# A feed-forward over a tree of 255 nodes: one merged table for the low levels, tiles in pairs, overflow groups of 128 rows

## The reference

```python
for _ in range(DEPTH + 1):                    # 8 levels, nodes 0 to 254
    score = einsum('td,td->t', flat_x, w1s[current]) + b1s[current]
    current = current * 2 + choice + 1        # choice: score > 0
path_weights = gelu(abs(logits))              # one weight per row and level
for i in range(DEPTH + 1):
    t_i = einsum('td,tdo->to', flat_x, w2s[nodes_i]) + b2s[nodes_i]
    out = out + t_i * path_weights[:, i][:, None]
```

## Time and profile before

| | |
|---|---|
| median of 3 runs | 547.82 us (547.79 to 549.1) |
| profiled execution | 548.32 us, its span 546.5 us |
| busy: PE, DVE, ACT, POOL | 378, 366, 300, 277 us |
| attention's last scores | near 338 us |
| first static product, first row-out | 412.6, 418.3 us |
| last row-out issued, end of span | 537.7, 546.5 us |

### The profile page before, as it was taken

How to read it: one execution, slowest core, us unless ns; L and a number is a source line. 1 busy time by engine, 2 the same in 40 slices (tenths; PEclk the granted TensorE clock), 3 DMA queues, 4 the chain that set the end, 5 groups by cost and what they waited for, 6 DMA issues and landing times.

```text
span 546.5 us, 8746 instructions
## 1 busy us (share of the span) xinstructions
PE 378.2 (69%) x3014; PEld 251.9 (46%) x3014; DVE 366.0 (67%) x594; ACT 299.8 (55%) x655; POOL 277.4 (51%) x315
## 2 busy tenths in 40 slices
PE   1333859888898988988588993556109996587780
PEld 1222525444465645655355651554007774354450
DVE  0644495878867789687888788625956999443341
ACT  2463767999888998889588694002001110254440
POOL 1456594322236287362677506838375777741211
PEclk9999996999999999999799996655558999599996
DMA  5202497397330333302331300750014110200000
GB/s 130 65 1 54 114 229 150 86 196 131 86 86 14 73 86 86 86 22 65 85 85 34 86 1 4 129 84 4 16 35 109 40 43 22 73 9 5 7 5 7
DMA packets 52029, 36.03 MB, mean 66 GB/s; under 512 B 25122, under 2 KB 50687, under 8 KB 51980
## 3 DMA queue, kind: packets, MB, share of 16 engines
q1 hardware_dynamic: 48238, 32.47, 27.4%
q0 software_dynamic: 2944, 2.45, 1.7%
q10 hardware_dynamic: 800, 0.49, 0.4%
HBM read 10.57 MB, written 8.79 MB: 35 GB/s over the span
## 4 chain that ended last, share of the span: by engine, by line
ACT 29%; PE 26%; DVE 25%; issue 8%; POOL 6%; DMA 3%; ACTq 0%; SPq 0%; POOLq 0%; DVEq 0%
ACT S L943 15%; PE S L735 5%; DVE nm L1097 5%; PE U L674 5%; DVE lm L1268 4%; DVE vT L1261 3%; ACT q L930 3%; ACT vT L930 3%; PE S L838 3%; ACT k L930 3%; DMA par<-in_L_tok_moving_var 2%; PE U L838 2%; POOL pool_a L459 2%; PE S L840 1%; POOL w L452 1%
## 5 line engine op out<-in xcount | busy, mean ns | idle before, releaser
L1097 DVE TENSOR_REDUCE nm<-S 128x1 f32<-128x748 f32 x192 | 171.9, 932 | 44.7 <-PE S L735 41.9
L943 ACT ACTIVATE S<-S,nm 128x748 f32<-128x748 f32 x192 | 167.1, 885 | 42.6 <-DVE nm L1097 41.4
L735 PE MATMUL S<-pool_a 128*128 128x512 f16 (+1 forms) x768 | 151.6, 332 | 29.6 <-ACT S L943 27.1
L735 PEld LDWEIGHTS S<-pool_a 128*128 128x128 f16 x768 | 68.9, 105 | 91.7 <-ACT S L943 56.2
L550 POOL DMA_INDIRECT out<-lm,vT x44 | 43.4, 985 | 58.1 <-DVE lm L1274 51.1
L459 POOL TENSOR_TENSOR pool_a<-q,pool_a 128x750 f16<-128x750 f32 x16 | 25.8, 1613 | 72.3 <-DVE pool_a L1064 72.1
L635 PE MATMUL U<-xhT,wq 128*128 128x250 f16 x288 | 42.9, 289 | 17.7 <-ACT q L930 8.2
L1268 DVE TENSOR_REDUCE lm<-vT 128x64 f32<-128x512 f32 x44 | 45.1, 1026 | 1.6 <-DVE vT L1261 0.5
L943 ACT ACTIVATION_READ_ACCUMULATOR S<-S,nm 128x1 f32 x192 | 44.0, 229 | 0.0
L635 PEld LDWEIGHTS U<-xhT,wq 128*128 128x128 f16 x288 | 27.1, 104 | 35.5 <-ACT q L930 13.7
L491 POOL DMA_INDIRECT sorted_rows<-xrow,slot x24 | 26.9, 1119 | 18.4 <-DVE slot L1183 10.3
(11 more groups left out here) (214 smaller groups left out, 681.6 us busy)
## 6 DMA issues: line engine op xcount, KB each, us to landing
pool_a<-pool_a SPq DMA_DIRECT2D x64, 187.5 KB, 3.0
pool_a<-pool_a SPq DMA_DIRECT2D x64, 93.8 KB, 2.8
sorted_rows<-zrow SPq DMA_DIRECT2D x1, 3864.0 KB, 22.3
vT<-sorted_rows SPq DMA_DIRECT2D x11, 276.0 KB, 3.7
w<-in_L_ffn_w2s SPq DMA_DIRECT2D x1, 2048.0 KB
lm<-in_x SPq DMA_DIRECT2D x4, 375.0 KB
pool_a<-in_L_ffn_w2s SPq DMA_DIRECT2D x1, 1024.0 KB
out<-lm,vT POOLq DMA_INDIRECT x44, 2.1
```

The source lines that it names most:

```text
L735: last = mm(S[n % 3][:, c0:c1], kst[:, u % 3, a, hd, START[t]:START[t] + P], qst[:, u % 3, hd, c0:c1], start=(a == 0), stop=(a == 1))
L943: sc_.activation(S[n % 3][:, 0:N], S[n % 3][:, 0:N], ACT.Exp, bias=nm[:, b % 2, j, i:i + 1], accum_out=sm[:, b % 2, j, i:i + 1]).then_inc( ...
L1097: v.tensor_reduce(nm[:, b % 2, j, i:i + 1], S[n % 3][:, 0:N], X, ALU.max, negate=True).then_inc(s_max, 1)
```

## The change

Rows, order of the sort and results stay. What differs:

- Overflow groups have 128 rows (`P`) instead of 32, so a group is a tile with one leaf. 96 groups stay provided for: 96 tiles, `SLOTS` from 7168 to 16384.
- Static and overflow tiles go in pairs: one load, one transpose step, one PSUM tensor of 1024 columns and one VectorE step for two tiles. Overflow blocks under an `If` are one pair: 48 of them.
- Levels 0 to 5 lie in one table `wlow` of 32 x 6 entries, level 6 in `w6` behind it (256 entries instead of 160, 15 transfers instead of 19, twice). A static tile has seven products (384, 2 x 64, 4 x 64 columns), an overflow tile three of full height (384, 64, 64). ACT's copies to `yv` are gone.
- The reduction over levels becomes three additions (4+4, 2+2, 1+1 levels).
- The fill goes in four pieces, behind the stacks of units 1 to 4; `w7` behind those of unit 5. `q32`, `k32`, `xhT` and `wq` move into `pool_a`; the low tables also wait for the last q-k product.
- POOL issues the writes of batch 2 ahead of the wait for the last scores and of the clearing, which covers 16,384 elements instead of 10,368.
- Transposes of a pair are issued one pair ahead, the first overflow pair's before the last static pair's products; PE's wait for the group numbers comes at the third pair.

```diff
-SLOTS = STAT + OVG * G
-ST_TILES, OV_TILES = STAT // P, OVG * G // P
+SLOTS = STAT + OVG * P
+ST_TILES, OV_TILES = STAT // P, OVG
+FILLS = 4
+ST_PAIRS, F_PAIRS = ST_TILES // 2, F_TILES // 2
+NODES5 = 2 ** 5
+LOWN = 6 * NODES5
...
-                if w == 1:
+                if 1 <= w <= FILLS:
                     sp.wait_ge(s_id, 2)
-                    sp.dma_start(rows.rearrange("(t p) c -> p t c", p=P),
-                                 zrow[:].unsqueeze(1).to_broadcast([P, F_TILES, RW])).then_inc(s_fill, 16)
-                if w == 4:
+                    fl = slice((w - 1) * F_TILES // FILLS, w * F_TILES // FILLS)
+                    sp.dma_start(rows.rearrange("(t p) c -> p t c", p=P)[:, fl, :],
+                                 zrow[:].unsqueeze(1).to_broadcast([P, F_TILES // FILLS, RW])).then_inc(s_fill, 16)
+                if w == FILLS + 1:
...
             sp.wait_ge(s_score, 2 * NT * NU)
+            sp.wait_ge(s_prod, NU)
...
+                for lv in range(6):
+                    n = 2 ** lv
+                    r = NODES5 // n
+                    m = D if src is wv else 1
+                    if n <= r:
+                        for i in range(n):
+                            sp.dma_start(tv[rows_, i * r:(i + 1) * r, lv, :],
+                                         src[:, n - 1 + i:n + i, :].to_broadcast([m, r, D])).then_inc(s_low, 16)
+                    else:
+                        for q in range(r):
+                            sp.dma_start(tv[rows_, q::r, lv, :], src[:, n - 1:2 * n - 1, :]).then_inc(s_low, 16)
...
+            load_rows(ST_PAIRS)
             groups = sp.value_load(nact[0:1, 0:1], min_val=0, max_val=OVG)
-            for k in range(ST_TILES // 4, F_TILES // 4):
-                with sp.If(groups > 4 * (4 * k - ST_TILES)):
-                    load_rows(k)
+            for m in range(ST_PAIRS, F_PAIRS - 1):
+                with sp.If(groups > 2 * (m - ST_PAIRS)):
+                    load_rows(m + 1)
...
+            own_slots(B - 2)
             pool.wait_ge(s_score, 2 * NT * NU)
-            link(gp.memset(wlow[D:P, :], 0.0))
+            link(gp.memset(pool_a[D:P, 0:n_low + 2 * NODES5 * D], 0.0))
             pool.sem_inc(s_zl, 1)
             pool.wait_ge(s_uf, unit_no[("o", B - 1, 1)] + 1)
             link(gp.memset(xsT[D:P], 0.0))
             pool.sem_inc(s_zl, 1)
-            own_slots(B - 2)
             own_slots(B - 1)
...
+            def overflow_pair(m):
+                leaves = [nc.tensor.value_load(lami[0:1, 2 * (m - ST_PAIRS) + t:2 * (m - ST_PAIRS) + t + 1],
+                                               min_val=0, max_val=LEAVES - 1) for t in range(2)]
+                pair_ready(m)
+                for t in range(2):
+                    y = y_banks(m)[:, 512 * t:512 * (t + 1)]
+                    xk = xsT[:, m % 3, t * P:(t + 1) * P]
+                    mm(y[:, 0:6 * D], xk, wlow[:, bass.ds((leaves[t] >> 2) * (6 * D), 6 * D)], start=True, stop=True)
+                    mm(y[:, 6 * D:7 * D], xk, w6[:, bass.ds((leaves[t] >> 1) * D, D)], start=True, stop=True)
+                    last = mm(y[:, 7 * D:8 * D], xk, w7[:, bass.ds(leaves[t] * D, D)], start=True, stop=True)
+                last.then_inc(s_y, 1)
...
             xs_T(0)
+            for m in range(ST_PAIRS):
+                if m == 2:
+                    pe.wait_ge(s_goff, 1)
+                xs_T(m + 1)
+                static_pair(m)
             groups = pe.value_load(nact[0:1, 0:1], min_val=0, max_val=OVG)
+            for m in range(ST_PAIRS, F_PAIRS):
+                with pe.If(groups > 2 * (m - ST_PAIRS)):
+                    if m + 1 < F_PAIRS:
+                        xs_T(m + 1)
+                    overflow_pair(m)
...
+            def weigh(m):
+                dve.wait_ge(s_gelu, m + 1)
+                dve.wait_ge(s_y, m + 1)
+                wk = xs[:, m % NX, :, C_W:C_H]
+                v.tensor_tensor(wy[:, m % 2], y_banks(m)[:].rearrange("p (t l o) -> p t l o", t=2, l=DEPTH),
+                                wk.unsqueeze(3).to_broadcast([P, 2, DEPTH, D]), ALU.mult).then_inc(s_wy, 1)
...
+            for m in range(ST_PAIRS):
+                weigh(m)
+                if m >= 1:
+                    levels_1(m - 1)
+                levels_4(m)
+                if m >= 1:
+                    add_residual(m - 1)
+                levels_2(m)
...
+            for m in range(ST_PAIRS, F_PAIRS):
+                with dve.If(groups > 2 * (m - ST_PAIRS)):
+                    weigh(m)
+                    levels_4(m)
+                    levels_2(m)
+                    levels_1(m)
+                    add_residual(m)
```

More of the change, by code:

```diff
@@ L358, in _ @@
             for k in range(ST_TILES - NO, ST_TILES):
                 sp.wait_ge(s_outr[k % NO], 16 * (k // NO + 1))
-            for m in range(ST_TILES // 4, F_TILES // 4):
-                with sp.If(groups > 4 * (4 * m - ST_TILES)):
-                    for k in range(4 * m, 4 * m + 4):
+            for m in range(ST_PAIRS, F_PAIRS):
+                with sp.If(groups > 2 * (m - ST_PAIRS)):
+                    for k in range(2 * m, 2 * m + 2):
                         sp.wait_ge(s_outr[k % NO], 16 * (k // NO + 1))
@@ L497, in own_slots @@
                 if b == 0:
-                    pool.wait_ge(s_fill, 16)
+                    pool.wait_ge(s_fill, 16 * FILLS)
                 pool.wait_ge(s_slot, b + 1)
@@ L556, in _ @@
                     scatter(FIRST + k, oslot, s_sego)
-            for m in range(ST_TILES // 4, F_TILES // 4):
-                with pool.If(groups > 4 * (4 * m - ST_TILES)):
-                    for k in range(4 * m, 4 * m + 4):
+            for m in range(ST_PAIRS, F_PAIRS):
+                with pool.If(groups > 2 * (m - ST_PAIRS)):
+                    for k in range(2 * m, 2 * m + 2):
                         rows_out(k)
@@ L848, in _, with pair_ready @@
-            pe.wait_ge(s_goff, 1)
-            xs_T(0)
-            for k in range(ST_TILES):
-                if k % 4 == 0 and k + 4 < ST_TILES:
-                    xs_T(k // 4 + 1)
-                tile_products(k)
-            groups = pe.value_load(nact[0:1, 0:1], min_val=0, max_val=OVG)
-            for m in range(ST_TILES // 4, F_TILES // 4):
-                with pe.If(groups > 4 * (4 * m - ST_TILES)):
-                    xs_T(m)
-                    pairs = load_leaves(4 * m)
-                    for k in range(4 * m, 4 * m + 4):
-                        pairs = overflow_products(k, pairs)
+            def pair_ready(m):
+                pe.wait_ge(s_xc, m + 1)
+                if m >= NY:
+                    pe.wait_ge(s_wy, m - NY + 1)
@@ new lines, in levels_1, with add_residual @@
+            def levels_1(m):
+                for k in range(2 * m, 2 * m + 2):
+                    if k >= NO:
+                        dve.wait_ge(s_outr[k % NO], 16 * (k // NO))
+                dve.wait_ge(s_s2, m + 1)
+                w = wy[:, m % 2]
+                v.tensor_tensor(yo_pair(m), w[:, :, 0, :], w[:, :, 1, :], ALU.add).then_inc(s_sl, 1)
+            def add_residual(m):
+                dve.wait_ge(s_sl, m + 1)
+                o = yo_pair(m)
+                v.tensor_tensor(o, o, xs[:, m % NX, :, C_H:C_ID], ALU.add).then_inc(s_yo, 1)
```

240 lines of the change are left out of this document (84 added, 156 removed).

## The result

The changed kernel takes **554.66 us** (median, 553.51 to 555.58) against 547.81 us for the kernel before in the same comparison: ratio 1.0117, 95% interval 1.0096 to 1.0138, so slower by about 1.2%. The prediction was 556.0. The profiled execution took 553.51 us around a span of 551.8, the one before 548.32 around 546.5, so in the traces there are 5.3 us to place.

The account below looks back on a forecast made before the run. Waits, not busy engines, bound it: GpSimd's queue, then TensorE's walk. First row-out +8.8, last overflow write +10.8, last row-out -0.7, end +8.2: span 554.7, plus 1.8 less 0.5 gives 556.0 us; range 542 to 571.

Parts of the forecast that it names:

- Slots of batch 3: Start of the stage: a VectorE operation stands still beside GpSimd's longer clearing, so the slots come 5.4 us later.
- The end of 12.4 us: Upper bound of the slots' delay, if VectorE's two-input operations also stood still beside the clearing: 12.4 us.
- First row-out at 427.1: GpSimd's first row-out, behind slots, loads, first tiles and VectorE's steps: 427.1 instead of 418.27, +8.8 us.
- The GpSimd loop: Alternating row-outs and overflow writes: same 36 instructions, 45.0 us, plus 2 (0 to 5) beside VectorE's sums; last overflow write 474.1.
- Step of 3.1 in the overflow pairs: Overflow stage: 14 steps between pairs at 3.1 us each (ends 2.8 and 3.9), together 43.4 us.
- The walk: End of kernel: TensorE steps over 33 unused blocks, fetching code, in 22 us, ending at 554.2; bounds 5 and 134 us.
- the span ends with that: Kernel before: TensorE's steps over three unused blocks, 3.4 to 5.0 us each until 546.0, set the end of the span.
- The +8.2 of the end: End of the span: TensorE's walk ends at 554.2 and the span at 554.7, +8.2 us on the kernel before.
- Rival 1: TensorE's queue: sequencing costs nothing, step 2.8 us, last row-out 532.8, total time 544.1 us, faster by 0.7%; chance 20%.
- Rival 2: Cheap walk at the end but step 3.1: last row-out 537.0, SyncE 547.0, total time 548.3 us, no change; chance 12%.
- Rival 3: Score units: the fills delay the stacks of units 4 to 6, +7 us on the forecast, 563; chance 12%.
- Rival 4: Walk at the end: every step over a block costs a fetch, 134 us instead of 22, total 668 us; chance 6%.

Follow-up runs that it names:

- experiment 2: Changed kernel with the clearing of pool partitions 64 to 127 moved from GpSimd to ScalarE: 549.46 us, 1.0015 to the kernel before.
- experiment 3: Changed kernel with batch 2's row writes put back behind GpSimd's clearings, the clearing keeping its new size: 551.70 us, 1.0055 to the kernel before.
- Experiment 7: Changed kernel with the three additions put back to one reduction in the 16 static pairs only: 550.22 us, 1.0037 to the kernel before.
- experiment 6: Kernel before with room for 48 overflow groups instead of 96, so no block is stepped over: 548.03 us, 0.9997 to the kernel before.
- experiment 4: Changed kernel with all 24 overflow writes of GpSimd issued before its first row-out: 543.35 us, 0.9905 to the kernel before.
- Experiment 5: Kernel before with all 24 overflow writes of GpSimd issued before its first row-out: 545.87 us, 0.9958 to the kernel before.
- experiment 9: Kernel before with room for 48 groups and all overflow writes first: 570.68 us, 0.9889 to a kernel before at 577.0 in that session.
- experiment 10: Changed kernel with six more indirect GpSimd writes into a table nobody reads: 591.19 us, 1.0250 to the kernel before in that session.
- experiment 1: Changed kernel with conditional code for 16 overflow blocks beyond the static pair instead of 47: 552.75 us, 1.0081 to the kernel before.
- experiment 8: Changed kernel with the clearing on ScalarE and overflow writes first: 537.52 us, 0.9799; with static-pair reduction too: 563.62 us (0.9777), repeated 535.85 us (0.9775).

## Why the prediction was right or wrong

- **Slots of batch 3, +5.4.** Right in place, cause and size: 5.5 us, and experiments 2 and 3 show the cause. The end of 12.4 us is out: two-input operations and a reduction ran beside the clearing as always. The rule of the Trainium skill (SBUF — State Buffer, § SBUF: two separate sides) by which the delay was 5.4 agrees with this trace, where L271 with its two SBUF inputs took 0.95 us beside the clearing.
- **First row-out at 427.1.** It came at 426.89, and 1.5 us later where TensorE's clock rose later.
- **The GpSimd loop, +2 for the additions.** The term was mis-sized: the loop took 49.3 us instead of 45.0, +4.2, inside the bounds of 0 to 5 and near their upper end. Experiment 7 gives the 4.4 back.
- **Step of 3.1 in the overflow pairs.** 3.07 measured, but the reason was half right. I had three bounds at 2.8 to 3.0, on VectorE, on TensorE's sequencer and in its array, and counted the stage on TensorE; VectorE's own chain (2.92 us busy, the rest between dependent sums) sets it, and GpSimd is stretched to the same 3.07. TensorE's last product ends at 527.5, 4.7 us before the predicted 532.2, since three pairs of PSUM banks let it run ahead of VectorE, which I forgot. First products 12 us after the last overflow write instead of 14.7 made up for part of the longer loop. Last row-out 538.50 for 537.0.
- **The walk.** For TensorE I had 22 us, and it took 15.6: four steps of 1.6 to 2.1 us where I had six or seven of about 3, the others 0.20 to 0.35, most 0.21. The instruction queue brought five packets of 16 KB in that time (525 to 542), which fits fetches. What failed is the step "the span ends with that". It was wrong for the kernel before (experiment 6), so also for the changed one: GpSimd's drain, which I put at 550.6, ended at 551.5, TensorE's walk at 541.5 instead of 554.2. The two lay 0.3 us apart in the trace of before, and I took TensorE's, the earlier one, for the cause. The +8.2 of the end should have been built from GpSimd: its 33 steps behind VectorE's last sum, or the end of its last row-out if that is later, and then its drain.
- **Rivals.** Rivals 1 and 2 let the walk of TensorE be cheap or hidden; for the span it was hidden. Rival 2 had the last row-out at 537.0 (538.5) and SyncE through at 547.0 (546.2), and still gave 548.3, since I let it end with SyncE and left out the drain that I had put at 550.6 a paragraph earlier; with it, it would have been the better forecast of the mechanism. Rival 1's step of 2.8 us did not occur. **Rival 3** (fills) falls: the fills take 15.2 us each beside the stacks, and the first scores of each unit come between 0.2 us earlier and 0.6 us later than before. **Rival 4** falls with 29 of 33 steps at 0.20 to 0.35 us, most at 0.21; the Trainium skill (Advanced Engine Details and Errata, § Control Flow Timing) gives about 108 ns for a compare-and-branch, half of the 208 measured.

So the sum of 556.0 came near 554.66 partly by luck. From the last row-out to the end I had 17.7 us (537.0 to 554.7) where the trace has 13.3 (538.50 to 551.8), and those 17.7 were built on the wrong queue; the last row-out itself I had 1.5 us too early, with a loop 2.2 too short. The errors partly cancel. The main finding, that the shorter overflow stage only pays for the late start, holds; experiments 2 and 4 show where the gain went: some 5 us to a clearing beside a compare, and some 11 to GpSimd's interleaved queue, which keeps the overflow pairs waiting until 476. Experiment 5 shows that the small groups lose much less to that queue, 2.7 us.

## What to carry to other kernels

When work moves to larger units, ask which queue hands them out: here the same 24 writes between row-outs held the start of the stage, and the gain appeared only when they went first. A clearing on GpSimd is not free beside small VectorE compares and casts; put it on an idle engine, or see that its new place has no victim either. If two engines end within a few tenths of a microsecond, the profile doesn't say which one holds the end: run the kernel without one of the two ends before building a sum on it.

## What the runs showed of the hardware

- A last drain on GpSimd ends 7.60 us (kernel before, and experiments 5, 6, 9 and 10) or 9.06 us (changed kernel, experiments 1 to 4, 7, 8) after the later of its own start and the last indirect transfer's end. What chooses between the two is open.
- GpSimd's sequencer walks on while its indirect transfers stand in line: in experiment 4 the drain was issued at 529.95 with row-outs starting until 531.13. In that run the 33 branches behind the backlog cost nothing.
- Beside VectorE's addition of two SBUF inputs an indirect transfer of GpSimd takes 1.29 to 1.48 us instead of 0.98; beside a GpSimd clearing a VectorE compare of 0.19 us takes up to 5.88.
- TensorE's clock rose at one of two moments some 3 us apart under the same instructions (about 420 in the changed kernel, about 423 in experiment 1), which moved the first row-out by 1.5 us.
- A step over a block, branch to branch, took GpSimd 0.15 us and TensorE 0.27, but for four steps of 1.6 to 2.1 us on TensorE.
